# A fused two-layer transformer kernel on one core: a subtraction moved from GpSimd to VectorE, a root moved from GpSimd to ScalarE, and new step orders

## The chip, the cores and the metric

The kernel is written in Bass and runs on one core of a Trainium2 chip. The metric is the device time of one execution in microseconds, lower is better. The five engines (TensorE, VectorE, ScalarE, GpSimd, SyncE) run their own instruction queues in order and meet only at semaphores.

## The reference

`x` has 16 batches of 256 rows with 256 values. Two layers are applied to it, each of the form `x + attention(norm(x)) + ffn(norm(x))`.

- Layer 0: causal attention with 16 heads of 16 values, and a gated feed-forward net of width 704 whose weights are integer codes less 128 times a scale: `down(silu(gate(x)) * up(x))`.
- Layer 1: attention in a latent space. For every head `c = x_h @ Wdkv.T` (64 values) is normalised to mean 0 and variance 1, `c = (c - mu) * rsqrt(var + 1e-5) * g + b`; scores, softmax and values come from `c`. The feed-forward net has a shared gated part (width 192) and 32 experts of width 96, of which each row takes its best 6.

## The kernel before

Nothing of the latent space is formed at its full width: small folded matrices stand in for it. So the normalisation of the keys needs only one number per row and head, `1 / sqrt(variance + eps)`. It is made in the tile `rt2` (128 x 32: two row halves by 16 heads) once a batch. The text calls it the key root. `dve2` multiplies a product from TensorE with the normalised rows (L1330), sums it to `rt2` (L1332), clips it and adds 64 eps (L1334), divides by 64 (L1336); `gp2` raises it to the power -0.5 on GpSimd (L817); `dve2` then spreads it over `rw2` (L1340), TensorE transposes that (L1793), and it scales the keys (L1344) and the values (L1356) of layer 1.

TensorE takes f16 operands. A value that must keep its precision is split in two f16 parts, high and low: ScalarE casts it to the high part, and the low part is the value less the high part. All gated products of the feed-forward nets go this way. There are 288 of them, numbered by `H3`: 6 chunks of layer 0's net a batch ("f"), 2 of the shared net a batch ("s"), and 160 expert units ("u"), each 64 to 128 rows of 256 values. For each one ScalarE does the tanh (L1135), VectorE gates it in two instructions (L1486, and L1490 or L1492) in the tile `th3`, ScalarE casts it to `h3h` (L1140), and GpSimd subtracts to `h3l` (L913); TensorE multiplies both parts with the down weights (L1636, L1633, L1950). `th3`, `h3h` and `h3l` have two buffers each; product n may write `h3l` only when TensorE is through with product n-2.

All work is written as streams of steps, generators that yield at the end of a step: stream 0 is the entry of layer 0 for a batch, 1 its attention, 2 its projection and the entry of layer 1 (with the key root), 3 the feed-forward work of all batches and units, 4 the sum over a row's experts, 7 the routing, 8 the attention of layer 1. Several batches are in flight at once. Which stream an engine serves next is written out by hand in `ORDERS`, one digit a step, for each of the five engines; an engine follows its digits in order, so a step whose data is not there holds up all behind it. The order of the feed-forward uses within stream 3 is `plan`. Its last 34 expert units come after all else; the sum over the experts of the last three batches follows them.

ScalarE uses two functions, Exp and Tanh, beside copies and casts. GpSimd also raises the variances of the two layer norms (L803), issues the scatters and gathers of the expert rows (L889, L933) and does a few sums (L821, L899, L907).

Of the kernel before, what the change touches and what calls it, by code (L numbers as in the profile page):

```python
# [40 lines left out]
def prev(it):  # L41
# [6 lines left out]
        "51111111115555555515555055551005555201111111110281030048111111111121082801008211131111111028800301111811111121"  # L48
        "02881302001181111111208810008331333111111111233333333333323333108833333033003333111111183311133233333313323308"
        "83331333320803303311111111133333321388333331338032333303300111111133113333323883333333108333333033331300333211"  # L50
        "11111113333333321348804333333103038230311331111111333233318833344033138333200033111311111133323334883133433380"
        "31333203300111111113314334338283333333183033334343333313003323301111133111143333438323813330333810330433203311"
        "11111113343333288133333333833313432433333323388333343343333338333333333333333333333333333343343333333333333343"
        "34333333333333334334333333333333834343334444401234678"
    ),
    "gp": (
        "55555553355333553355550555533333323322273300777333333233224007723777333333223233230037773773333332320023237773"
        "77332323233323300777773333332323323323333333007737373373333333333223323233377333007733733332233233332377377337"
        "33333300333332323233233773377337333330033334344344344343443344323232332337733300773373443443344433443232432332"
        "44433773773333730043444344433444232443233342337733773734434334340044344344344322332334423773377337343443443433"  # L60
        "34400434433443443443444433443433323232344443277337773343340043444344433333232324444323443477373737343443444333"
        "33343444324234244334434443773327733734333333333444344344434443433344344344434434443433344344344434434443433344"
        "344344434434443433343444444444444444444444444444444444444440012345677"
    ),
    "act": (
        "75555675567653733353533357335335111151171115115115171150115150173503330733333333727223227727333770011111071131"
        "13011170113133113731113313337888888888888788888888271118112121811132121111200331130111013033333338883288388888"
        "38882238882882888328111338113100111013113011103111131313333333888888888828881118811828281188118212113112138311"
        "38110011033300333233322388838828882888388288888888333838000111101111101111111111118883383383338338833883338333"
        "88233338833238338832833383282333323333333333383331113811311300131331311301131333113033113133130333333333333333"  # L70
        "33333388833883383283838838283233838383283211881138281338113313811383113113313131113133100333033333033303332388"
        "83388323833882388388833233828338838388323833338338111311313331131131131113111113133333333333333388833008383083"
        "88308833808832333883383888332238383323323323338333833333333333333333333331113311311300331311331310118881033113"
        "33113133133338833038338838833388833333883838823883833322333332323332338338311133113111111133113130031130111331"
        "33333033303333333388383238838338833232838833882323882888338883333833833111313133111111131131331131131313333000"
        "33303303888388233838838332832833883233238823833883883833833338333333311131133113113133111111131131888318833838"
        "83880038303883038338038233883282333838333283233333283333333333333333333333333333118883133113311300131881018188"
        "13131333311331133133133033330388338383383333883332838833338833228333823233833233333333111111131111131131333311"
        "33130011313030388830883833388388338338338283338383328823388823233332383338333333311131131133113131133113131313"
        "11331331338838883833883338833383882333888828288832332333323833383333333333333333333333333333333333333333333388"  # L80
        "33888888333333333333333333883333333833333883333333333333333333333338833333333833333333333333338833333333883333"
        "333383333333333333333333333338333333338333333333333330011234788"
    ),
    "dve": (
        "11615516551155611111131131115513135533553550155000550135503533332112232121121127112112112117131131001770070888"
        "08830883888838818838738311113111111111111111811282232822002720072213037077018838888888888888878331133131121121"
        "12121131218112121712318228300300700378807881388738888388188118878131111311311111111111228322200200272832182370"
        "10337887880887388388888888287223211321272311218211111312138113811001710010708878878808888888888718111133133113"
        "13328223211332122373211223118131113113833007003038870773133880338818888838811881381381711311131311131321122123"
        "12183223722238383700313788700738018883880838888388807383232221131312111212183117113111321121831283737388773881"  # L90
        "88888888818838783333003003030303283112213212322372382211381137313178878838871138818811881838181181733380000303"
        "33010333414344343443113841411312142112132114123121213173211822318437338800887700371038808833818838808838783443"
        "43424113221321141213112121813112112117321844413843474378838738873881888880088388173003800304434324442232114432"
        "12321181217231131414121184318141311713378878738888883888888818733434100004340430348034442432242431121328237328"
        "11227313114113117771388183881881818883883881181378443434344003004430344403133443410443434438434432431122132131"
        "21182128311721322711311414131141777888888883883883881800300847480434104434034343383211221321311211212732118122"
        "31184431147114413148378877388888838888188387384443144433333283223244422432738244233844437444323878877838888388"
        "88888873833333333334434443443443444333384434443443443444333344344434434434443333844344438443443444333444444444"
        "444444444444444444444444444001123478"
    ),  # L100
    "pe": (
        "61116116113113111113131313133333113111111111111111001110133103033333333332221111211332311272112111111111300011"
        "81818101883110118831880118831188133881833171831313133111118118131818118118118181818888282118111128112133211232"
        "17111210001011101331880888888888888887833333338328111138118211831188138121811218128281238338312811811371100011"
        "01131011883118810388313811818818818888378331111311313111311813181181188218828118118821182118211281233113118123"
        "18110007110133308883838808888888882878233332338283111288281882188211881181318133811381318117100008811108811818"
        "81810881188188188117181111111833338111333838113383138333823832338113833832381323282332311323113831133131138313"
        "33311811371130001131313188011331131331880331131331880188338838838388383311171831313311313331138113383183283113"
        "28113838238132833282181213811233813811381333811731131131188113133100083188388088383838838830837833033238328338"
        "33821111831812811383121382113383181311821381338132833811371133113131188131311881118818818181831883188338378333"  # L110
# [15 lines left out]
def program(nc, a, out):  # L126
# [29 lines left out]
    with ctx:  # L156
# [736 lines left out]
        def gp3(gp):  # L893
            g = nc.gpsimd
            for use in plan:
                if use[0] == "whole":
# [3 lines left out]
                    yield  # L900
                if use[0] != "in":
                    continue
                n, at = H3[use[1:]], use[1:]
# [1182 lines left out]
```

## Time and profile before

| what | us |
|---|---|
| median of 3 runs | 2054.55 |
| lowest and highest run | 2050.47 and 2056.04 |
| the profiled execution, its own time | 2047.37 |
| its span, first to last instruction | 2045.5 |
| TensorE busy in it | 1523.8 |
| VectorE busy | 1123.0 |
| GpSimd busy | 940.2 |
| ScalarE busy | 877.0 |

The profile is of one execution. A busy share counts the time in which an engine works on an instruction, not in which it is held by one that waits; the waits stand beside the instructions, with what ended them. PE is TensorE, PEld its weight loads, DVE VectorE, ACT ScalarE, POOL GpSimd, SPq the DMA issues of SyncE. The mean granted clock of TensorE was 0.887 of its full 2.4 GHz.

### The profile page before, as it was taken

The page shows a single profiled execution, that of the slowest core. Times are in us where ns is not written, and L with a number is a line of the kernel's source. Part 1 is how long each engine was busy: PE and PEld are TensorE (multiplying, and loading weights), DVE is VectorE, ACT ScalarE, POOL GpSimd, SP SyncE. Part 2 cuts the span into 40 slices and gives each one's busy share as a digit, 9 for nine tenths or more (in the row PEclk, how much of TensorE's full clock was granted, in tenths as well). Part 3 has the DMA queues.
Part 4 walks back from the last instruction along what each step waited for, and adds up shares of the span by engine and source line. Part 5 has one row for each costly group of instructions (what it writes and reads, how often), then busy time and mean ns, then how long its engine had stood idle before and what let it go on. Part 6 is the DMA issues. An engine that isn't in the chain of part 4 may idle for free.

```text
span 2045.5 us, 46039 instructions
## 1 busy us (share of the span) xinstructions
PE 1523.8 (74%) x15344; PEld 1146.5 (56%) x15344; DVE 1123.0 (55%) x2910; ACT 877.0 (43%) x1789; POOL 940.2 (46%) x1246
## 2 busy tenths in 40 slices
PE   3755857787788887887878777797977877788840
PEld 2433545554466666676666656565764666566630
DVE  5565556657555655556465656566555555524332
ACT  2441433353355454553544444453643545355520
POOL 3335062534425154425336455546646456625555
PEclk8777988899899999998999988898998989899975
DMA  6986641413334425353344535364463644546643
GB/s 151 238 212 170 152 112 22 112 45 93 99 87 130 111 90 124 110 125 101 102 105 136 116 122 132 117 144 123 134 150 105 140 127 110 162 125 187 190 141 93
DMA packets 467085, 258.04 MB, mean 126 GB/s; under 512 B 231537, under 2 KB 454321, under 8 KB 466865
## 3 DMA queue, kind: packets, MB, share of 16 engines
q1 hardware_dynamic: 399696, 178.00, 33.8%
q0 software_dynamic: 22784, 54.55, 9.6%
q10 hardware_dynamic: 44384, 22.55, 3.9%
q8 instruction: 140, 2.29, 0.5%
q14 instruction: 81, 0.66, 0.1%
HBM read 127.28 MB, written 127.40 MB: 125 GB/s over the span
## 4 chain that ended last, share of the span: by engine, by line
PE 38%; issue 15%; DVE 14%; POOL 10%; another core or an unknown queue 6%; DMA 5%; SPq 3%; ACT 3%; DVEq 0%; ACTq 0%; POOLq 0%
PE s3r L1636 11%; POOL rt L817 4%; PE s2m L1636 4%; POOL yard L933 2%; PE s3r L1939 2%; PE s1b L1706 2%; PE s3r L1963 2%; SPq L652 2%; DVE th L1486 2%; DMA yard<-y_d,slot 2%; PE s2r L1814 2%; DVE mx L1285 2%; POOL h3l L913 2%; DVE m L1366 1%
## 5 line engine op out<-in xcount | busy, mean ns | idle before, releaser
L913 POOL TENSOR_TENSOR h3l<-th,h3h 96x256 f16<-96x256 f32 (+2 forms) x288 | 199.2, 693 | 602.7 <-ACT h3h L1140 600.1
L1486 DVE SCALAR_TENSOR_TENSOR th<-th,s3r 96x256 f32<-96x256 f32 (+2 forms) x288 | 119.4, 415 | 288.1 <-ACT th L1135 259.8
L933 POOL DMA_INDIRECT yard<-y_d,slot x192 | 192.6, 1003 | 85.8 <-issue 39.9
L1140 ACT CAST h3h<-th 96x256 f16<-96x256 f32 (+2 forms) x288 | 116.5, 405 | 247.8 <-DVE th L1492 124.0
L889 POOL DMA_INDIRECT rows_d<-rows,slot x192 | 188.1, 980 | 67.7 <-issue 66.8
L1366 DVE TENSOR_REDUCE m<-s2r 128x3 f32<-128x384 f32 x256 | 135.4, 553 | 151.2 <-remote 99.3
L1636 PE MATMUL s3r<-yard,xg 128*128 128x128 f16 x1920 | 183.1, 227 | 46.8 <-DVE th L1492 20.6
L1127 ACT COPY yard<-s3r 128x1024 f16<-128x1024 f16 x160 | 162.2, 1014 | 63.1 <-remote 36.4
L1636 PE MATMUL s3r<-yard,xu 128*128 128x128 f16 x1920 | 181.1, 225 | 3.0 <-issue 2.9
L1636 PEld LDWEIGHTS s3r<-yard,xg 128*128 x1920 | 133.0, 101 | 77.4 <-issue 63.6
L1135 ACT ACTIVATE th<-s3r 96x256 f32<-96x256 f32 (+2 forms) x192 | 72.8, 379 | 217.7 <-PE s3r L1636 179.8
L1522 DVE SCALAR_TENSOR_TENSOR yard<-yard,share 128x256 f32<-128x256 f32 x192 | 101.8, 530 | 95.5 <-DMA yard<-y_d,slot 89.1
L1636 PEld LDWEIGHTS s3r<-yard,xu 128*128 x1920 | 135.5, 100 | 12.1 <-issue 3.6
L1090 ACT ACTIVATE weights<-s2r 128x384 f32<-128x384 f32 x256 | 113.9, 489 | 55.6 <-PE s2r L1859 54.5
L1636 PE MATMUL s3r<-xd,h3h 96*128 x640 | 123.0, 287 | 12.4 <-POOL h3l L913 9.0
L1814 PE MATMUL s2r<-stacks 126*128 126x128 f16 (+1 forms) x512 | 94.2, 276 | 46.5 <-issue 26.8
L1963 PE MATMUL s3r<-ident,yard 128*128 128x128 f16 x1280 | 102.6, 225 | 17.5 <-DVE th L1490 9.7
L1027 ACT ACTIVATE weights<-s1a 128x512 f32<-128x512 f32 x144 | 86.3, 599 | 67.0 <-PE s1b L1706 39.8
L1147 ACT COPY yard<-s3r 128x512 f32<-128x512 f32 x160 | 92.9, 581 | 37.4 <-PE s3r L1636 23.6
L817 POOL TENSOR_TENSOR rt<-rt,less_half 128x32 f32<-128x32 f32 x16 | 86.9, 5434 | 40.3 <-DVE rt L1336 40.2
L1963 PEld LDWEIGHTS s3r<-ident,yard 128*128 128x128 f16 x1280 | 86.2, 101 | 29.3 <-issue 25.7
L1285 DVE TENSOR_REDUCE mx<-s1b 128x2 f32<-128x512 f32 x128 | 87.3, 682 | 12.6 <-PE s1b L1688 11.9
(326 smaller groups left out, 3705.0 us busy)
## 6 DMA issues: line engine op xcount, KB each, us to landing
yard<-rows_d SPq DMA_DIRECT2D x160, 256.0 KB
y_d<-yard SPq DMA_DIRECT2D x160, 256.0 KB
rows_d<-share ACTq DMA_DIRECT2D x21, 1024.0 KB, 6.8
part_d<-part SPq DMA_DIRECT2D x32, 512.0 KB, 3.6
stacks<-part_d SPq DMA_DIRECT2D x192, 64.0 KB
land<-part_d SPq DMA_DIRECT2D x96, 64.0 KB
part<-part_d SPq DMA_DIRECT2D x96, 64.0 KB
x<-in_L_attn_x SPq DMA_DIRECT2D x16, 256.0 KB, 2.6
```

The source lines that it names most:

```text
L817: g.tensor_tensor(rt2[:, :, :], rt2[:, :, :], less_half[:, :].unsqueeze(2).to_broadcast([P, T, H]), ALU.pow).then_inc(sem("root2"), 1)
L889: g.indirect_dma_start(rows_d[k % 2][:, :], bass.IndirectOffsetOnAxis(ap=slot4[:, it, t, j:j + 1], axis=0), rows2[:, t, :, :].rearrange("p ...
L913: g.tensor_tensor(h3l[0:m, n % 2, :], th3[0:m, n % 2, :], h3h[0:m, n % 2, :], ALU.subtract).then_inc(sem("low3"), 1)
L933: g.indirect_dma_start(got4[:, n % RING4, :], None, y_d[k][:, :], bass.IndirectOffsetOnAxis(ap=slot4[:, b, t, j:j + 1], axis=0)).then_inc( ...
L1127: s.copy(xt3[:, r % 2, :, :, :].rearrange("p i g n -> p (i g n)"), bk[:, :].bitcast(F16)).then_inc(empties3(use), 1)
L1140: s.copy(h3h[0:m, n % 2, :], th3[0:m, n % 2, :]).then_inc(sem("high3"), 1)
L1285: v.tensor_reduce(mx1[:, h, :], two(bk), AX.X, ALU.max).then_inc(empties1(u), 1)
L1366: v.tensor_reduce(m32[:, h, :], bk[:, 0:3 * P].rearrange("p (c n) -> p c n", n=P), AX.X, ALU.max).then_inc(empties2(u), 1)
L1486: v.scalar_tensor_tensor(h, h, 1.0, bk[0:m, 0:2 * P], ALU.add, ALU.mult).then_inc(sem("gate3"), 1)
L1636: ins = nc.tensor.matmul(bk, lhs[i][k], rhs[j][k], start=first, stop=last)
L1814: mm(bk[:, P * j:P * j + P * (j + 1)], query(qst2, h, OPEN)[:, P * j:P * j + P], key(kst2, h, OPEN)[:, 0:P * (j + 1)], start=j == 0, stop= ...
L1963: ins = nc.tensor.transpose(bk[:, 512 * i + P * k:512 * i + P * k + P], rows3[:, r % 2, i, P * k:P * k + P], ident16[:, :])
```

## The change

Three things, and new orders for all five engines.

- The low part of the gated products is made by VectorE, as a step of its own behind the gate's step, in place of GpSimd.
- The key root: VectorE's division by 64 goes (ScalarE's activation scales by 1/64 itself), ScalarE takes the square root in place of GpSimd's power, and VectorE takes the reciprocal.
- `ORDERS`: GpSimd has 304 steps fewer (288 low parts, 16 roots), VectorE 288 more, ScalarE 16 more. All five strings are new. `plan` is the same.

```diff
@@ ORDERS @@
-    "sp": ( ... 713 steps ... ), "gp": ( ... 729 ... ), "act": ( ... 1823 ... ), "dve": ( ... 1576 ... ), "pe": ( ... 2197 ... )
+    "sp": ( ... 713 steps ... ), "gp": ( ... 425 ... ), "act": ( ... 1839 ... ), "dve": ( ... 1864 ... ), "pe": ( ... 2197 ... )
@@ gp2 @@
-            gp.wait_ge(*event("var2_made", it, 1))
-            g.tensor_tensor(rt2[:, :, :], rt2[:, :, :], less_half[:, :].unsqueeze(2).to_broadcast([P, T, H]), ALU.pow).then_inc(sem("root2"), 1)
-            yield
@@ gp3 @@
-                m = rows_of(at)
-                gp.wait_ge(*event("high3", None, n + 1))
-                if n >= 2:
-                    gp.wait_ge(*weighed3(n - 2))
-                g.tensor_tensor(h3l[0:m, n % 2, :], th3[0:m, n % 2, :], h3h[0:m, n % 2, :], ALU.subtract).then_inc(sem("low3"), 1)
-                yield
@@ act2, between the copy of x2h and the routing's Exp @@
+            act.wait_ge(*event("var2_made", it, 1))
+            s.activation(rt2[:, :, :], rt2[:, :, :], ACT.Sqrt, scale=1.0 / L).then_inc(sem("root2"), 1)
+            yield
@@ dve2 @@
-            v.tensor_scalar(rt2[:, :, :], rt2[:, :, :], 0.0, L * EPS, ALU.max, ALU.add).then_inc(sem("var2_scaled"), 1)
-            dve.wait_ge(*event("var2_scaled", it, 1))
-            v.tensor_scalar(rt2[:, :, :], rt2[:, :, :], 1.0 / L, None, ALU.mult).then_inc(sem("var2_made"), 1)
+            v.tensor_scalar(rt2[:, :, :], rt2[:, :, :], 0.0, L * EPS, ALU.max, ALU.add).then_inc(sem("var2_made"), 1)
             yield
             dve.wait_ge(*event("root2", it, 1))
+            v.reciprocal(rt2[:, :, :], rt2[:, :, :]).then_inc(sem("rs2_made"), 1)
+            dve.wait_ge(*event("rs2_made", it, 1))
             dve.wait_ge(*event("row_low", it, 1))
             v.tensor_copy(rw2, rt2[:, :, :].unsqueeze(3).to_broadcast([P, T, H, HD])).then_inc(sem("rs2_made"), 1)
@@ dve3, behind the gate @@
+                    dve.wait_ge(*event("high3", None, n + 1))
+                    if n >= 2:
+                        dve.wait_ge(*weighed3(n - 2))
+                    v.tensor_tensor(h3l[0:m, n % 2, :], h, h3h[0:m, n % 2, :], ALU.subtract).then_inc(sem("low3"), 1)
+                    yield
@@ pe2 @@
-            pe.wait_ge(*event("rs2_made", it, 1))
+            pe.wait_ge(*event("rs2_made", it, 2))
```

## Rows read from the trace of the kernel before

**Rows 1.** The page's busy time by engine, with instruction counts.

```profile
PE 1523.8 (74%) x15344; PEld 1146.5 (56%) x15344; DVE 1123.0 (55%) x2910; ACT 877.0 (43%) x1789; POOL 940.2 (46%) x1246
```

**Rows 2.** The page's chain that ended last, by engine and by line.

```profile
PE 38%; issue 15%; DVE 14%; POOL 10%; another core or an unknown queue 6%; DMA 5%; SPq 3%; ACT 3%; DVEq 0%; ACTq 0%; POOLq 0%
PE s3r L1636 11%; POOL rt L817 4%; PE s2m L1636 4%; POOL yard L933 2%; PE s3r L1939 2%; PE s1b L1706 2%; PE s3r L1963 2%; SPq L652 2%; DVE th L1486 2%; DMA yard<-y_d,slot 2%; PE s2r L1814 2%; DVE mx L1285 2%; POOL h3l L913 2%; DVE m L1366 1%
```

**Rows 3.** Windows by stage: length, then busy us of each engine, PEclk, DMA, GB/s.

```profile
500.00:1000.00 500.00, 410.64 (x4339) 319.28 (x4338) 284.33 (x754) 237.69 (x490) 197.61 (x297) 0.93 0.38 105
1000.00:1500.00 500.00, 405.61 (x4237) 311.70 (x4234) 291.15 (x765) 235.85 (x489) 258.92 (x334) 0.92 0.49 129
1750.00:1980.00 230.00, 175.29 (x1936) 139.70 (x1936) 80.93 (x190) 109.83 (x206) 111.78 (x142) 0.93 0.56 164
```

**Rows 4.** The tile rt: durations ns (min/median/max), and who waited for its writers.

```profile
L1336 DVE TENSOR_SCALAR rt<-rt x16: 181/182/425, 157.5 to 1727.5; 128x32 f32<-128x32 f32 x16
L817 POOL TENSOR_TENSOR rt<-rt,less_half x16: 5419/5424/5513, 157.7 to 1728.0; 128x32 f32<-128x32 f32 x16
...
  DVE xn L1340: 75.5, 16
```

**Rows 5.** Timeline of one key root: start, us, what, idle before and its releaser.

```profile
809.42 0.18 DVE L1336 TENSOR_SCALAR rt<-rt 128x32 f32<-128x32 f32 x1
...
809.68 5.42 POOL L817 TENSOR_TENSOR rt<-rt,less_half 128x32 f32<-128x32 f32 x1 [5.79 <-DVE rt L1336]
...
815.14 0.43 DVE L1340 COPY xn<-rt 128x512 f32<-128x512 f32 x1 [4.94 <-POOL rt L817]
...
816.22 0.11 PEld L1686 LDWEIGHTS s1b<-kst,qst 126*128 126x128 f16 x2 [4.80 <-DVE mx L1285]
```

**Rows 6.** Windows, each root's start to 3 us behind its end: first, last, sum.

```profile
157.74:166.18 8.44, 4.49 (x52) 3.77 (x50) 3.58 (x16) 1.10 (x3) 5.43 (x1) 0.89 0.36 103
...
1728.00:1736.44 8.44, 3.98 (x48) 3.38 (x46) 3.28 (x16) 3.27 (x7) 7.91 (x4) 0.89 0.30 93
sum 135.04, PE 67.90 PEld 51.02 DVE 52.31 ACT 34.85 POOL 99.12; mean PE 4.24 PEld 3.19 DVE 3.27 ACT 2.18 POOL 6.20
```

**Rows 7.** By line, xcount | busy us, mean ns | idle before; then the stage window of h3l.

```profile
L913 POOL TENSOR_TENSOR h3l<-th,h3h 96x256 f16<-96x256 f32 (+2 forms) x288 | 199.2, 693 | 602.7 <-ACT h3h L1140 600.1 <-issue 1.1
...
L1140 ACT CAST h3h<-th 96x256 f16<-96x256 f32 (+2 forms) x288 | 116.5, 405 | 247.8 <-DVE th L1492 124.0 <-DVE th L1490 109.7 <-issue 9.8
...
1750.00:1980.00 230.00, 33.31 (x47) 0.93 0.56 164
```

**Rows 8.** Nearest prices: lines L1537, L1396, L1239, L1070, then ScalarE's first two instructions.

```profile
L1537 DVE TENSOR_TENSOR shd<-stacks,shd x1: 407/407/407, 67.1 to 67.1; 64x256 f16<-64x256 f32 x1
...
L1396 DVE RECIPROCAL sc<-el x16: 552/553/554, 163.8 to 1734.1; 128x64 f32<-128x64 f32 x16
...
L1239 DVE RECIPROCAL rc<-s2r x32: 235/248/258, 243.0 to 1940.2; 128x16 f32<-128x16 f32 x32
...
L1070 ACT ACTIVATE el<-s2m x16: 223/223/230, 159.0 to 1728.8; 128x64 f32<-128x64 f32 x16
...
0.80 1.28 ACT L1157 ACT_TABLE_LOAD   x1 [0.80 <-PEq L2076]
6.56 1.47 ACT L1157 CAST wqkv<-yard 128x1536 f16<-128x1536 f32 x1 [4.48 <-DMA yard<-in_L_attn_w_qkv]
```

**Rows 9.** TensorE's waits from 180 to 1750 us: us in total, times, longest.

```profile
PE s1b L1726 <- ACT weights L1027: 28.1, 16, 6.1
...
PE s1b L1686 <- DVE mx L1285: 14.0, 10, 4.8
```

**Rows 10.** Timeline of one expert unit among the last 34.

```profile
1859.94 0.40 ACT L1140 CAST h3h<-th 96x256 f16<-96x256 f32 x1 [0.94 <-DVE th L1492]
...
1860.43 0.67 POOL L913 TENSOR_TENSOR h3l<-th,h3h 96x256 f16<-96x256 f32 x1 [3.60 <-ACT h3h L1140]
...
1862.76 0.10 PEld L1636 LDWEIGHTS s3r<-xd,h3l 96*128 96x128 f16 x1
...
1863.08 0.42 DVE L1486 SCALAR_TENSOR_TENSOR th<-th,s3r 96x256 f32<-96x256 f32 x1 [3.17 <-issue]
```

More of the change, by code:

```diff
@@ new lines @@
+        "31883333330330013333111111121138333331332338803333303300331331111118233111333333323388013330330803331113311111"
+        "31123333333334433123088333303300331331111113823111333441333323883330331483230400331111311111333233338833133344"
+        "30383310302301111131131413348332338333333013833303003333133111111121133333833314423383333330133323380330011313"
+        "11114113342333388331333333334338413332348433323383333333333333333333333383333333333333334334333333333333433433"
+        "33333383333433433333333333333433433333334444401234678"
@@ L69 @@
[L69 to L73, printed above, removed]
@@ new lines @@
+        "30113701331133113137331111311778888888788888882118188881181212181182211321112110011313031303303333333332888888"
+        "88228882882328888888280080338301111013113311313111113311313113313888888882888882882888881122831211121181133001"
+        "13811010113113013133333333388828888888282888828288328811181233181001381101110111011111188833388333323383388333"
+        "32332883338388332388233238883388323333383333333833383333111333333311330033113333133311333113113301331313113313"
+        "31333030333333333332333333888388233283888828388233882382388338833833330038338311131133331131131311031133101131"
@@ new lines @@
+        "13310331333333333333333333333233888388388822883838822883281188138832813138333118113133113331131333003303330333"
+        "11303113133133333333333333333388823388388832882338388322883382883388238333833383333333311313113311311100110111"
+        "00111113313333338883338838333388338833833883333238838333883388223833323233233323833311138113113331310031311301"
+        "11033333110331311333133333333333333333888388238888832823883388283338832111332881181323181313138131311331333113"
+        "11131333000333303308883288333888388332328388328832833883238832833333833338333333331113311331133111311331131331"
@@ new lines @@
+        "13111331330088888088808833380883388332838838833833232833338323232332333333333333333333333333333331113130013110"
+        "11101888311031133331133118831338133883388383883883338388338833823833328233333223211111332131313131333113113133"
+        "31313133131313333333330033303303330328883388338883883282388338823828832882383333833383333333333111311331313311"
+        "31333111313313331131133131333888338838338838838388388328888882282382333233233333333333333333333333333333333333"
+        "33333333333333333333333333333333888333388333383883338833338333333333883333883383388338833338333333333333333383"
@@ new lines @@
+        "38228330370077887881888888888188118178111111111333333233322233323323821373323112333321313813131833333333003730"
+        "03303337377333883388310333338130333883883883883883838723111323211231311212111213138721321311330032003831103833"
+        "33733388377730388180338333138811388318883883118313871131311313123131221121123238127323228383373333388300880078"
+        "70387330833813033338313883118818838338713113131313132322232332382731322323811383111137131313388388300877373380"
+        "03388088088880881783131131331313413143431131314343383124443223443231141231321142137332831232384344334003743004"
@@ L902, in gp3 @@
                     continue
-                n, at = H3[use[1:]], use[1:]
+                at = use[1:]
                 if at[0] == "s" and at[2] == 0:
```

101 lines of the change are left out of this document (40 added, 61 removed), and 4 rows, old and new, of the table PER.

## The prediction

> **What bounds the kernel now.** I read the busy shares first: TensorE leads with 74%, VectorE has 55%, and GpSimd and ScalarE are below half [rows 1]. No engine is full, so I went on to the chain that ended last. TensorE has 38% of it, VectorE 14%, GpSimd 10%, ScalarE 3%, and 15% is issue [rows 2]. GpSimd's part matters here: the key root's power alone is 4%, some 82 us, and the low part h3l is 2%, some 41 us.
>
> The windows by stage split the run. From 500 to 1500 us, where batches overlap, TensorE is busy 0.82 of the time, VectorE 0.57, ScalarE 0.47 [rows 3]. From 1750 to 1980 us only expert units are left, and VectorE falls to 0.35. Behind 1980 us is the last sum over experts, which has no gated product and no root.
>
> So in the overlapped stage TensorE is the nearest to a bound, and the rest is in-order queues waiting for one another. What the change is worth is what it does to the queues of VectorE and ScalarE in that stage.
>
> **The root: what goes.** The power takes 5.42 us on GpSimd, 16 times, and VectorE stands still for 75.5 us in front of the copy L1340 that needs it [rows 4]. The timeline shows the damage: VectorE idles 4.94 us, the score maxima L1285 stand behind it, and TensorE, whose bank they free, waits 4.80 us [rows 5].
>
> How much of a stall turns into time? In the 16 windows from a root's start to 3 us behind its end, 135.0 us in all, TensorE was busy 67.9 us [rows 6]. At the 0.82 of the stage around it would have been busy 110.7. It lost 42.8 us of work, which at 0.82 is 52 us of time, for 75.5 us of VectorE's stall: 0.69 us per us. I use that ratio as what a microsecond costs in which VectorE's queue is held at its worst place. These windows include the lower clock there (PEclk 0.89 in both shown, against 0.93 and 0.92 in the stage) [rows 3, 6].
>
> **The root: what comes.** VectorE loses one instruction of 0.18 us [rows 4] and gains a reciprocal of 128x32. The same operation takes 0.248 us at 16 elements and 0.553 at 64 [rows 8]; between them, 0.35 us at 32. Net +0.17 us, 3 us in 16 batches. ScalarE gains a square root of 128x32; its activation of 128x64 takes 0.22 us [rows 8], so about 0.20, 3 us in all.
>
> The trace has one table load in the whole run, 1.28 us, although Exp and Tanh alternate all the way [rows 8]: they share a table. I take it that Sqrt does not, which no row shows. Then each batch has two more loads, one ahead of the root and one ahead of the next Exp or Tanh: 32 x 1.28 = 41 us of ScalarE.
>
> VectorE's wait is then: 0.08 us hop to ScalarE (as from L1336 to L817 in [rows 5]), 0.3 us for what ScalarE is at, 1.28 load, 0.20 root, 0.05 back: 1.9 us against 75.5/16 = 4.7. That saves 2.8 x 16 = 45 us of stall, less 3 for the reciprocal: 42. At 0.69 it is **-29 us**. Bounds: if the load runs ahead of the wait, as the first one did (it ended at 2.08, the data came at 6.56 [rows 8]), the wait is 0.6 us and the gain 63 x 0.69 = 44 us; if ScalarE comes late by an exponential or two and has to empty first, the wait is 3.3 us and the gain is 14 us. I take the middle, since ScalarE is busy about half of the stage.
>
> The Trainium skill (ScalarE: Activation LUTs, "What ACT_TABLE_LOAD costs" and "Table sets") states that exp and tanh are in one set and sqrt in another, that a switch is a 1283 ns load plus a drain of about 1380 ns, and so advises against alternating exp and sqrt. The 1.28 us row agrees with the load; no run here shows the drain yet. By its 2.66 us the root's wait would be 3.3 us and ScalarE's extra 85 us in place of 41, and that sum would give about 20 to 30 us more than mine.
>
> **The tables' cost to ScalarE's own queue.** 41 + 3 = 44 us are added to 877. Behind them stand the exponentials, and TensorE waits for those already, 28.1 us at one line alone [rows 9]. Lower price: ScalarE's share of the chain, 3% of 2045 = 61 us for 877 busy, 0.07 us per us. Upper: 0.69, as for a held queue. ScalarE is idle half of the stage, so nearer the lower end: 0.25, **+11 us** (3 to 30).
>
> **The low part: what moves.** GpSimd loses 199.2 us [rows 7]. VectorE has done exactly this operation once, f32 less f16 to f16 of 64x256 from SBUF, in 0.407 us [rows 8], and 288 of them are 117 us. 47 lie in the stage of units alone [rows 7], where VectorE next has a gate 2 us later and TensorE reads h3l 1.7 us after GpSimd has finished it [rows 10]: these cost nothing. 241 x 0.407 = 98 us remain in the overlapped stage.
>
> The new step waits for ScalarE's cast in VectorE's queue, where before GpSimd had the wait (600.1 us of it, free of charge [rows 7]). In the new order of VectorE, of the 244 low steps ahead of the end stage, 49 follow their gate at once, 99 with one step between, 96 with more. At once means a hop, the cast's 0.405 us and a hop, 0.5 us each, 25 us; with one step of about 0.39 us (1123 us by 2910 instructions [rows 1]) some 0.2 us are left, 20 us. Behind the waiting instruction stand the score maxima, and TensorE waits for them (14.0 us at one line already [rows 9]).
>
> So VectorE's queue gets 98 + 45 = 143 us longer in a stage in which it is 0.57 busy. Lower price: its share of the chain over its busy time, 14% of 2045 = 286 by 1123, 0.25 us per us, gives 36. Upper: 0.69, gives 99. New orders can place much of it well, but the waits are of the same kind as the root's, so I take 0.4: 57 us. Against it stands the chain's 41 us of L913, which come back at 0.407/0.693: -17. Together **+40 us** (19 to 82). With no cast waits at all it would be +8.
>
> GpSimd's gathers and scatters no longer stand behind low parts. This I cost at nothing: the gathers wait for saved units, and the last 66 us hold no low part.
>
> **Sum.** -29 + 11 + 40 = +22 us on the profiled execution: own time 2047.4 to 2069, span 2045.5 to 2067. That execution was 7 us faster than the median shown; on the median the sum gives 2076, and I write 2075. SyncE's and TensorE's digits are new too; what they do as such I can't price and it widens the range by some 10 us each way.
>
> **Rivals.**
>
> *A, the root wins (faster).* The load runs ahead of the root's wait, and the low parts sit in VectorE's idle time. For it: VectorE is idle 0.43 of the stage, and all 16 powers lie on the chain. Against: 148 of 244 low steps have at most one step between. -44 + 3 + 8 = -33: 2022 us. It decides when a microsecond of VectorE's added work costs under about 0.25 and the root's wait is under 1.5 us.
>
> *B, they cancel.* The root's wait is as in my sum, VectorE's price is the chain's 0.25: -27 + 8 + 19 = 0: 2054 us.
>
> *C, the tables cost more than their loads.* ScalarE reaches the root late, empties, loads, and its exponentials stand behind. The wait is 3.3 us, the root saves 14, ScalarE's extra is 64 us (a further 0.6 us, one exponential's length, per switch) at 0.69, 44 us, and the low part +40: +70, 2125 us. For it: the order has Exp and Tanh on both sides of nearly every root. Against: ScalarE has 3% of the chain. The Trainium skill's drain, cited above, is this mechanism.
>
> **Chances.** My forecast 0.38 (its own range 2062 to 2095), A 0.30, B 0.18, C 0.14. The range that holds 8 in 10 is 2020 to 2115: it takes in A's centre and half of C. Within 0.3% (6 us, about what the runs shown, 2050 to 2056, can tell from no change) is B, 0.18; slower is the forecast and C, 0.52; faster is A, 0.30.
>
> **What would show it.** Right: 33 table loads of 1.28 us; VectorE's wait before the reciprocal near 1.9 us, 30 us in all against 75.5; h3l on VectorE at 0.41 us and 117 us; VectorE near 1240 us busy, GpSimd near 654, ScalarE near 921; waits of VectorE for the cast L1140 of 30 to 60 us; TensorE's share of the stage down from 0.82. Wrong: if no further table load stands in the trace the root's gain nears 44 us; if VectorE's waits for the cast are small and TensorE's waits for L1285 shrink, A holds; if TensorE waits for exponentials behind the loads more than 60 us, C.

## The result, and the profile after

The changed kernel takes 2027.54 us at the median of 4 runs (2020.76 to 2031.42), the kernel before on the same chip 2055.3 us (2050.47 to 2058.01). The ratio is 0.9864, with an interval from 0.983 to 0.9898: **28 us faster**. The prediction had said 2075 us and slower; its range of 2020 to 2115 holds the time. The profiled execution's own time is 2020.76 us, its span 2018.9.

Busy time and the chain that ended last, of the changed kernel's page, for comparison with [rows 1, 2]:

```profile
PE 1508.2 (75%) x15344; PEld 1127.1 (56%) x15344; DVE 1205.5 (60%) x3198; ACT 916.0 (45%) x1837; POOL 664.5 (33%) x942
...
PE 40%; DVE 19%; issue 10%; another core or an unknown queue 9%; DMA 6%; ACT 5%; SPq 3%; POOL 2%; DVEq 0%; ACTq 0%; POOLq 0%
PE s3r L1634 12%; PE s2m L1634 4%; PE s3r L1937 3%; DVE m L1359 3%; PE s3r L1961 2%; DVE mx L1278 2%; DMA yard<-y_d,slot 2%; PE s2r L1854 2%; DVE th L1479 2%; SPq L651 2%; PE s1b L1704 2%; POOL yard L923 1%; PE s3r L1948 1%; PE s2r L1812 1%
```

The work moved as foreseen (ScalarE 921, GpSimd 654 and VectorE 1240 were named; VectorE has 1205.5). GpSimd's share of the chain fell from 10% to 2%, and VectorE's rose from 14% to 19%.

The tile rt after (durations min/median/max; then who waited for its writers), which answers to [rows 4]:

```profile
L1057 ACT ACTIVATE rt<-rt x16: 229/229/231, 155.8 to 1696.0; 128x32 f32<-128x32 f32 x16
L1330 DVE RECIPROCAL rt<-rt x16: 341/345/353, 156.9 to 1696.3; 128x32 f32<-128x32 f32 x16
L1333 DVE COPY xn<-rt x16: 426/427/474, 157.3 to 1696.7; 128x512 f32<-128x512 f32 x16
...
  ACT rt L1057: 7.1, 2
  DVE rt L1330: 5.6, 6
```

VectorE's 16 waits for the root, 75.5 us before, are 6 waits of 5.6 us in all. The prediction had 30. The timeline of one root after (start, us, what, idle before) shows why, beside [rows 5]:

```profile
911.68 0.59 ACT L1140 COPY yard<-s3r 128x512 f32<-128x512 f32 x1
...
911.93 0.18 DVE L1327 TENSOR_SCALAR rt<-rt 128x32 f32<-128x32 f32 x1
912.02 0.41 DVE L1490 TENSOR_TENSOR h3l<-th,h3h 96x256 f16<-96x256 f32 x1
912.29 1.28 ACT L1057 ACT_TABLE_LOAD   x1
...
912.63 0.62 DVE L1239 TENSOR_TENSOR on<-s2r,rc 128x64 f32<-128x64 f32 x4
...
913.58 0.23 ACT L1057 ACTIVATE rt<-rt 128x32 f32<-128x32 f32 x1
...
913.83 1.28 ACT L1063 ACT_TABLE_LOAD   x1
913.84 0.35 DVE L1330 RECIPROCAL rt<-rt 128x32 f32<-128x32 f32 x1 [0.59 <-ACT rt L1057]
914.23 0.43 DVE L1333 COPY xn<-rt 128x512 f32<-128x512 f32 x1
...
1692.42 1.28 ACT L1057 ACT_TABLE_LOAD   x1
...
1696.04 0.23 ACT L1057 ACTIVATE rt<-rt 128x32 f32<-128x32 f32 x1 [2.34 <-DVE rt L1327]
```

The new order puts a low part and a few short steps between the variance and the reciprocal, so the load and the root lie beside VectorE's work. Table loads are there as foreseen, 33 of 1.283 us, two for each root; in the last batch the load ran ahead of the wait, 2.3 us before the data came.

Windows after: two of the 16 from a root's start, their sum, then the stage (length, busy us of TensorE, its weight loads, VectorE, ScalarE, GpSimd, PEclk, DMA, GB/s), beside [rows 3, 6]:

```profile
155.83:164.27 8.44, 6.53 (x61) 4.89 (x59) 5.82 (x23) 2.57 (x5) 0.00 (x0) 0.94 0.61 174
...
1696.07:1704.51 8.44, 6.90 (x81) 5.70 (x78) 6.65 (x29) 5.70 (x12) 0.66 (x1) 0.99 0.51 159
sum 135.04, PE 115.82 PEld 88.89 DVE 101.77 ACT 98.70 POOL 17.07; mean PE 7.24 PEld 5.56 DVE 6.36 ACT 6.17 POOL 1.07
...
500.00:1000.00 500.00, 412.91 (x4488) 319.95 (x4487) 308.57 (x844) 259.68 (x524) 126.23 (x215) 0.95 0.43 114
1000.00:1500.00 500.00, 404.37 (x4310) 309.60 (x4308) 326.70 (x887) 250.82 (x511) 184.91 (x268) 0.92 0.48 127
```

TensorE is busy 115.8 of the 135.0 us around the roots, where it had 67.9 [rows 6]: the hole is gone. In the two stage windows its busy share is that of before, 0.82, but they hold 8798 of its instructions in place of 8576 [rows 3], 2.6% more in the same 1000 us, at a granted clock of 0.95 in place of 0.93 in the first. The busy share hid the gain; the count of instructions shows it.

The low part after (the tile h3l: what wrote it, and what VectorE waited for), then TensorE's waits for the score maxima:

```profile
L1490 DVE TENSOR_TENSOR h3l<-th,h3h x288: 360/416/1920, 72.0 to 1943.2; 96x256 f16<-96x256 f32 x80, 128x256 f16<-128x256 f32 x56, 64x256 f16<-64x256 f32 x8
...
  ACT h3h L1133: 50.5, 78
```

```profile
PE s1a L1684 <- DVE mx L1278: 7.7, 12, 1.5
...
PE s1b L1684 <- DVE mx L1278: 2.2, 6, 0.9
```

The cast waits are 50.5 us, the 30 to 60 foreseen, and yet TensorE waits less for the maxima, 2.2 us where one line had 14.0 [rows 9].

### The profile page after: what moved, and what is told of

It is laid out like the page before. It is cut to its first block, busy times and chain, and to the rows that moved or that the text cites. A ratio compares the mean times of both kernels' runs of the same rounds, so it can differ in the third digit from the quotient of the medians.

```text
span 2018.9 us, 46071 instructions
## 1 busy us (share of the span) xinstructions
PE 1508.2 (75%) x15344; PEld 1127.1 (56%) x15344; DVE 1205.5 (60%) x3198; ACT 916.0 (45%) x1837; POOL 664.5 (33%) x942
## 4 chain that ended last, share of the span: by engine, by line
PE 40%; DVE 19%; issue 10%; another core or an unknown queue 9%; DMA 6%; ACT 5%; SPq 3%; POOL 2%; DVEq 0%; ACTq 0%; POOLq 0%
PE s3r L1634 12%; PE s2m L1634 4%; PE s3r L1937 3%; DVE m L1359 3%; PE s3r L1961 2%; DVE mx L1278 2%; DMA yard<-y_d,slot 2%; PE s2r L1854 2%; DVE th L1479 2%; SPq L651 2%; PE s1b L1704 2%; POOL yard L923 1%; PE s3r L1948 1%; PE s2r L1812 1%
## 5 line engine op out<-in xcount | busy, mean ns | idle before, releaser
L1359 DVE TENSOR_REDUCE m<-s2r 128x3 f32<-128x384 f32 x256 | 134.1, 551 | 133.6 <-remote 82.3
L1490 DVE TENSOR_TENSOR h3l<-th,h3h 96x256 f16<-96x256 f32 (+2 forms) x288 | 125.3, 435 | 54.0 <-ACT h3h L1133 50.5
L802 POOL TENSOR_TENSOR mv<-mv,less_half 128x2 f32<-128x2 f32 x32 | 24.1, 752 | 395.8 <-DVE mv L1218 395.6
L1520 DVE SCALAR_TENSOR_TENSOR yard<-yard,share 128x256 f32<-128x256 f32 x192 | 95.1, 495 | 86.1 <-DMA yard<-y_d,slot 77.2
L1812 PEld LDWEIGHTS s2r<-stacks 126*128 126x128 f16 x512 | 44.4, 103 | 110.1 <-DVE m L1359 51.1
L1854 PE MATMUL s2r<-stacks 128*128 128x256 f16 (+1 forms) x512 | 74.4, 254 | 34.6 <-ACT yard L1092 13.1
```

Source lines behind the costliest of these rows:

```text
L1359: v.tensor_reduce(m32[:, h, :], bk[:, 0:3 * P].rearrange("p (c n) -> p c n", n=P), AX.X, ALU.max).then_inc(empties2(u), 1)
L1490: v.tensor_tensor(h3l[0:m, n % 2, :], h, h3h[0:m, n % 2, :], ALU.subtract).then_inc(sem("low3"), 1)
L1812: mm(bk[:, P * j:P * j + P * (j + 1)], query(qst2, h, OPEN)[:, P * j:P * j + P], key(kst2, h, OPEN)[:, 0:P * (j + 1)], start=j == 0, stop= ...
L1854: mm(ring2[u % 2][:, at:at + S - P * j], key(kst2, h, FULL)[:, P * j:P * j + P], query(qst2, h, FULL)[:, P * j:S], start=j == 0, stop=Fals ...
```

## The experiments

Each was timed in 5 rounds beside the kernel before on the same chip. Microseconds are the ratio's distance from 1 by 2054.55. Two theories stood against each other at first: *prices*, that my terms had the wrong size, and *orders*, that the new orders made the gain. "Old orders" are those of before with the moved steps put in and nothing else moved: the low parts at the times where they had run, the root's step on ScalarE right ahead of the routing's Exp.

**The root.** `cheap_pow` is the kernel before with a multiplication for the power, so the root's value is left out:

```diff
-  g.tensor_tensor(rt2[:, :, :], rt2[:, :, :], less_half..., ALU.pow).then_inc(sem("root2"), 1)
+  g.tensor_tensor(rt2[:, :, :], rt2[:, :, :], less_half..., ALU.mult).then_inc(sem("root2"), 1)
```

> The kernel before with the power on GpSimd replaced by a multiplication of the same shape (the key root's value is left out). Nothing else changes, the orders stay. Root theory (a held VectorE queue costs 0.69 us per us): VectorE's wait before L1340 falls from 75.5 us to about 8 us, and the time by 45 us (35 to 55), to a ratio of 0.978. Orders theory (the gain of the change came from the new orders): under 15 us. Low-part theory (the gain came from the low part): under 15 us.

Measured: 0.9586 [0.9551, 0.9621], 85 us faster. The tile rt of that kernel (the durations, then who waited):

```profile
L817 POOL TENSOR_TENSOR rt<-rt,less_half x16: 238/239/336, 156.6 to 1651.5; 128x32 f32<-128x32 f32 x16
...
  POOL rt L817: 1.1, 3
```

VectorE's wait went from 75.5 to 1.1 us, 74 us for 85 us of time: **1.14 us per us, not 0.69**. The same edit takes 83 us off GpSimd (16 times 5.424 less 0.239), about what the chain in [rows 2] had for the power, 4% or 82 us. This run doesn't separate what VectorE's stall cost from what GpSimd's held queue cost.

`root_only` is the kernel before with the diff's hunks of gp2, act2, dve2 and pe2 alone, in the old orders. `root_no_sqrt` is the same with no table switch; it leaves the root out:

```diff
-  s.activation(rt2[:, :, :], rt2[:, :, :], ACT.Sqrt, scale=1.0 / L).then_inc(sem("root2"), 1)
+  s.activation(rt2[:, :, :], rt2[:, :, :], ACT.Identity, scale=1.0 / L).then_inc(sem("root2"), 1)
```

> The kernel before with the key root alone moved to ScalarE with a reciprocal; in the orders GpSimd's root steps are dropped and a step for ScalarE is put right ahead of the routing's Exp, all else stays. Root theory: 32 more table loads, VectorE's wait 10 to 30 us instead of 75.5, and 25 to 45 us faster, as much as the whole change or more (ratio about 0.983). Orders theory: about 0 to 10 us. Low-part theory: under 10 us.

> The root moved alone in the old orders, with Identity in place of Sqrt (the square root is left out), so that no table is switched. If the loads cost in the old orders what lies between the cheap power (0.9586) and the root moved alone (0.9774): a ratio near 0.960, 30 to 40 us under the root moved alone. If they are hidden as in the changed kernel (where leaving them out gave 0.9867 against 0.9864): 0.975 to 0.980, and the difference comes from where ScalarE's step stands.

Measured: `root_only` 0.9774 [0.9735, 0.9814], 46 us faster; `root_no_sqrt` 0.9635 [0.9604, 0.9666], 75 us. VectorE's wait for the root, first of `root_only`, then of `root_no_sqrt`:

```profile
  ACT rt L1064: 20.8, 13
```

```profile
  ACT rt L1064: 8.0, 8
```

The root away from GpSimd is worth 75 us, and the table loads take 29 back. By 1.14 the 12.8 us of longer wait would be 15 of these (an estimate); 14 are left for ScalarE's own queue, where I had 11.

`after_no_sqrt` makes the same edit in the changed kernel.

> The changed kernel with Identity in place of Sqrt (the square root is left out), so that no table is switched; the orders and all else stay. If the 32 loads (41 us of ScalarE) are hidden, as ScalarE's 0.07 us per us of the chain has it: 0 to 5 us faster than the changed kernel (2028). If they hold ScalarE's queue as the root held VectorE's: 25 to 40 us faster (about 1995), which is what lies between the cheap power (1970) and the root moved alone (2007).

Measured: 0.9867 [0.9842, 0.9892] against 0.9864 for the changed kernel. In the new orders the 32 loads cost nothing that shows; the intervals would hide some 9 us.

`pow_late` is the kernel before with VectorE's order sorted anew, so that the copy (L1340) comes about 4 us later by the profile's times. In half of the batches that puts 1 to 3 more steps ahead of it, and in all 224 of VectorE's 1576 steps stand in another place.

> The kernel before with both parts on GpSimd; in VectorE's order the step that needs the root is put 4 us later by the profile's times, as far as the other engines' orders allow (another 0 to 3 steps go ahead of it in half of the batches). If VectorE's order was what made the power a stall: 15 to 40 us faster than before. If the chain over the power itself decides, since TensorE's order goes through the root: under 10 us.

Measured: 1.0089 [1.0055, 1.0123], 18 us slower, though VectorE's wait fell from 75.5 to 68.6 us. A step put off shortens the wait and can lengthen the chain through the root. With so many steps moved the run doesn't show that this is the cause; it shows that a shorter wait there is no gain by itself.

**The low part.** `low_only` is the kernel before with the hunks of gp3 and dve3 alone; `both_simple` has both moves, in the old orders.

> The kernel before with the low part alone moved to VectorE; its steps stand in VectorE's order where GpSimd began them in time in the profile before, all other digits stay. Root theory: slower by 8 to 40 us (my prediction had 40, the result of the change points to 10 to 20), ratio about 1.007. Low-part theory (GpSimd's slow and blocked low part was the loss): faster by 15 to 30 us. Orders theory: slower by more than 30 us, since it takes new orders to hide it.

> The kernel before with both moves and the two simple edits of the orders together, without the new orders. Root theory: the sum of the two, 15 to 30 us faster, near the change itself (ratio 0.986 to 0.993). Orders theory: no faster than before or slower, the whole gain is missing. Low-part theory: faster by 25 us, of which the low part gives most.

Measured: 1.0249 [1.0214, 1.0283], 51 us slower, and 1.0035 [1.0012, 1.0058]. So the low part costs 51 us alone and 54 on top of the root, and the new orders, from `both_simple` to the changed kernel, give back 1.7%, **35 us**. That comes out of two comparisons, each with before, and it takes in whatever is poor in my own placing of the steps: against a better placing in the old orders it would be less. From `root_only` to the changed kernel, low part and new orders together, it is 18 us of loss.

`after_low_twice` makes each low part a second time on VectorE; `after_low_tiny` and `both_low_tiny` make 8 of its 256 columns. The rest is not zero as the expectation has it: the zeroing stands ahead of the start of the kernel, which uses the same memory for constants, and what that wrote stays.

```diff
+  v.tensor_tensor(h3l[0:m, n % 2, :], h, h3h[0:m, n % 2, :], ALU.subtract).then_inc(sem("twice3"), 1)
+  dve.wait_ge(*event("twice3", None, n + 1))
   v.tensor_tensor(h3l[0:m, n % 2, :], h, h3h[0:m, n % 2, :], ALU.subtract).then_inc(sem("low3"), 1)
...
-  v.tensor_tensor(h3l[0:m, n % 2, :], h, h3h[0:m, n % 2, :], ALU.subtract).then_inc(sem("low3"), 1)
+  v.tensor_tensor(h3l[0:m, n % 2, 0:8], h[:, 0:8], h3h[0:m, n % 2, 0:8], ALU.subtract).then_inc(sem("low3"), 1)
```

> The changed kernel with every low part computed twice on VectorE, the second behind the first; the orders stay. It prices VectorE's work in its queue: 288 x 0.42 = 121 us and some 0.05 us between. At 0.25 us per us (VectorE's share of the chain): 30 us slower than the changed kernel. At 0.4, my prediction's price: 50 us. At 1.0, as the root's stall was worth by the cheap power: 120 us.

> The changed kernel with a low part of 8 columns of 256 on VectorE (the other columns are left zero), so that the step, its waits and its place stay and 0.26 us of its work go, 75 us in all. At the 0.24 us per us that computing it twice gave: 18 us faster than the changed kernel, a ratio near 0.977. At 0.4: 30 us, 0.971.

> Both moves in the old orders (both_simple, 1.0035) with the same low part of 8 columns. If the low part's cost in the old orders is VectorE's work: 18 to 30 us faster than both_simple, 0.989 to 0.995, most of the way back to the root alone (0.9774). If it is that its steps stand badly in the old orders, where they wait for casts and hold what is behind: under 10 us faster, above 0.998.

Measured: twice 1.0007 [0.9982, 1.0031], 29 us above the changed kernel for 120 us more of VectorE's busy time, 0.25 us per us. Tiny 0.9837 [0.9805, 0.9869] and 0.9994 [0.9975, 1.0013], 6 and 8 us below their parents for about 70 us less, 0.1 us per us; the 6 are not clear of the intervals, the 8 barely. The work's price is about 0.1 to 0.25, not the 0.4 that I took.

`after_no_cast_wait` and `both_no_cast_wait` make the low part as the gated value less itself (zero), so VectorE reads no cast and waits for none; TensorE waits for it.

```diff
-  dve.wait_ge(*event("high3", None, n + 1))
+  dve.wait_ge(*emptied3(use))
...
-  v.tensor_tensor(h3l[0:m, n % 2, :], h, h3h[0:m, n % 2, :], ALU.subtract).then_inc(sem("low3"), 1)
+  v.tensor_tensor(h3l[0:m, n % 2, :], h, h, ALU.subtract).then_inc(sem("low3"), 1)
@@ pe3, three places @@
+  pe.wait_ge(*event("high3", None, n + 1))
```

> The changed kernel with a low part that does not read the cast (the gated value less itself, so the low part is zero), so that VectorE waits only for its own gate; TensorE waits for the cast itself. It prices the wait for the cast, 50.5 us in 78 waits in the changed kernel. If these waits cost what they last: 30 to 50 us faster than the changed kernel, a ratio near 0.965. If they lie in slack: under 10 us, 0.982 to 0.986.

> The kernel before with both moves in the old orders (2065.73 us, ratio 1.0035), but each low part is computed as the gated value minus itself (zero), so VectorE does not read the cast and does not wait for ScalarE there; TensorE waits for the cast itself. The low part is left out of the result. Theory A, the waits of VectorE for the cast (47.9 us, 72 of them) are what the low part costs in the old orders: 25 to 45 us faster, a ratio of 0.982 to 0.991. Theory B, GpSimd's emptied queue: about 1.003. Theory C, the low part's place in VectorE's order: 0.998 to 1.003, since the steps stay where they are.

Measured: 0.9836 [0.9807, 0.9865] against 0.9864, and 1.0036 [1.0016, 1.0056] against 1.0035. **The cast waits, 45 us in my sum, cost about 6 us in the new orders, which the intervals can't tell from nothing, and nothing in the old ones.**

**GpSimd's emptied queue.** VectorE's 120 us of work are 12 to 30 of the 54 us by these prices, the waits nothing. The rest had no owner. `both_gp_busy` is `both_simple` with GpSimd doing a subtraction of the same size on constants, behind the same cast, at each old place of a low part:

```diff
+  gp.wait_ge(*event("high3", None, H3[use[1:]] + 1))
...
+  g.tensor_tensor(spare[0:m, :], sd_row[0:m, :], wgate[0:m, 0, 0:E], ALU.subtract).then_inc(sem("idle_low"), 1)
+  yield
```

> The kernel before with both moves in the old orders (2065.73 us, ratio 1.0035), and GpSimd keeps the queue that it had with the low part: in its place it does a subtraction of the same size on constants into a spare tile. Theory B, that scatters and gathers which now run earlier disturb the rest: 25 to 45 us faster, a ratio of about 0.985. Theory A, the waits for the cast: unchanged at about 1.003, since these stay. Theory C, the place of the steps in VectorE's order: unchanged too.

Measured: 0.9905 [0.9888, 0.9921]. **288 useless instructions on GpSimd make the kernel 27 us faster.** From `root_only` (0.9774) to it is VectorE's side of the low part, 27 us; from it to `both_simple` is the emptied queue, 27 us. The two are not quite separate: with GpSimd's subtractions beside them VectorE's own low parts take 0.505 us in the mean in place of 0.435, and VectorE is busy for 40 us more than in `both_simple`. VectorE runs its instructions in the same order in both, so I set them side by side: the later start does not grow evenly but jumps, 12.3, 8.8, 8.7, 6.8 and 6.6 us at five steps of L1359. The timeline of `both_simple` at the first of these:

```profile
1665.20 0.96 POOL L885 DMA_INDIRECT rows_d<-rows,slot  x1 [0.30 <-issue]
1665.39 0.42 DVE L1485 TENSOR_TENSOR th<-s3r,th 96x256 f32<-96x256 f32 x1
...
1671.53 0.96 POOL L885 DMA_INDIRECT rows_d<-rows,slot  x1 [0.30 <-issue]
1672.79 0.97 POOL L885 DMA_INDIRECT rows_d<-rows,slot  x1 [0.30 <-issue]
1673.13 0.60 ACT L1017 ACTIVATE weights<-s1b 128x512 f32<-128x512 f32 x1 [8.22 <-remote]
...
1673.78 0.61 PE L1724 MATMUL s1b<-qst,kst 128*128 128x256 f16 x2 [8.90 <-ACT weights L1017]
...
1678.06 0.56 DVE L1359 TENSOR_REDUCE m<-s2r 128x3 f32<-128x384 f32 x1 [12.24 <-issue]
```

And the window of that stretch, then the one of `both_gp_busy` at the same place:

```profile
1665.85:1673.10 7.25, 0.00 (x0) 0.00 (x0) 0.00 (x0) 0.00 (x0) 5.42 (x7) 0.50 0.27 94
```

```profile
1636.55:1643.80 7.25, 4.58 (x42) 3.10 (x40) 2.47 (x6) 3.06 (x5) 5.84 (x7) 1.00 0.39 129
```

For 7.25 us no instruction of TensorE, VectorE or ScalarE stands in the trace. The views name no instruction that held them: VectorE's next one has "issue" as its releaser, ScalarE's has "remote", an event that they put down to nothing in the trace. GpSimd issues scatters all the while, 1.27 us from one to the next; TensorE's clock falls to 0.50, its lower level of 1.2 GHz.

The trace's semaphore events go further than the views. The ends of TensorE's matmuls in a profile are modelled, but the event by which a matmul tells the others that it is through is a record of its own. ScalarE starts at 1673.13, 0.08 us behind the event of a matmul whose end stands at 1661.91. In the longest stretch of the changed kernel (shown below) the events of four matmuls whose ends stand at 1719.40 to 1720.73 come at 1731.63 to 1731.81, and ScalarE and VectorE, which wait for two of them, start at 1731.65 and 1731.70. Elsewhere such an event lies 0.01 us behind the end (the median, for each of the three engines). **So in the still stretches VectorE and ScalarE wait for TensorE, whose matmuls report up to 12 us late there.** In `both_simple` 141 of TensorE's events are 1.5 to 20 us late, and in 139 of these delays GpSimd issues a gather or scatter. All eight kernels of the table below have the same 15344 matmuls in their traces, so missing records are not the reason.

With low-part steps between some scatters (`both_gp_busy`, at 1641.39) the same stretch runs on. It does so already over the four scatters from 1636.41 to 1640.41, which follow one another as closely, so scatters in a row are not enough by themselves.

```profile
1640.41 0.96 POOL L889 DMA_INDIRECT rows_d<-rows,slot  x1 [0.30 <-issue]
1641.39 0.69 POOL L912 TENSOR_TENSOR spare<-sd_row,wgate 96x256 f16<-96x256 f32 x1
1642.25 0.99 POOL L889 DMA_INDIRECT rows_d<-rows,slot  x1 [0.17 <-issue]
```

I counted such stretches ahead of the last gate in each trace: over 1.5 us without an instruction of the three engines, with at least two indirect issues under way in them. Beside them stands the time in which an event of TensorE was due by its matmul's end and over 1.5 us late, overlaps counted once.

| kernel | ratio | still stretches | us in them | us with a late event |
|---|---|---|---|---|
| before | 1 | 10 | 33.9 | 202 |
| `root_only` | 0.9774 | 8 | 33.0 | 208 |
| `both_gp_busy` | 0.9905 | 9 | 27.8 | 198 |
| `low_only` | 1.0249 | 16 | 57.9 | 237 |
| `both_simple` | 1.0035 | 15 | 64.9 | 240 |
| `both_no_cast_wait` | 1.0036 | 13 | 50.3 | 230 |
| `both_low_tiny` | 0.9994 | 12 | 40.6 | 226 |
| the changed kernel | 0.9864 | 13 | 54.3 | 266 |

They come with the emptied queue: the three kernels in which GpSimd has a subtraction for each product have the least of both, and between `both_simple` and `both_gp_busy` it is 37 us of still stretches for 27 us of time. But they don't follow the time one to one: `both_low_tiny` has 24 us less of them than `both_simple` and gained 8. The changed kernel still has 54 us, the longest of them here:

```profile
1720.80:1731.60 10.80, 0.00 (x0) 0.00 (x0) 0.00 (x0) 0.00 (x0) 8.06 (x9) 0.63 0.42 148
```

**The new orders with the old placement.** `after_root_gp`, `after_low_gp` and `after_both_gp` give the root, the low part, or both back to GpSimd in the changed kernel, each step where its data had been ready. The other engines keep their order, less or plus the moved steps. GpSimd's own order is sorted anew, so its other steps change places too, which the expectations don't say. `after_low_gp2` and `after_both_gp2` put GpSimd's scatters 8 and 16 us later in its order.

> The changed kernel with the root back on GpSimd (the power), its steps in GpSimd's order at the times at which ScalarE began the square root; all other digits stay. Additive theory (root, low part and orders each have their own worth): 45 to 55 us slower than the changed kernel, about 2077. Rival, the new orders hide a slow root: under 20 us slower.

> The changed kernel with the low part back on GpSimd, its steps in GpSimd's order at the times at which VectorE began them; VectorE's low steps go, all other digits stay. Additive theory: 40 to 55 us faster than the changed kernel, 1975 to 1988. Fit theory (the new orders only make up for what the low part costs): 15 to 25 us faster, the same as the root moved alone in the old orders (2007).

> The new orders alone: root and low part both on GpSimd as in the kernel before, in the changed kernel's orders. Additive theory: 25 to 40 us faster than the kernel before (about 2022). Fit theory: the orders are worth nothing without the low part on VectorE, 2045 to 2070.

> As after_low_gp (the changed kernel with the low part back on GpSimd), but GpSimd's scatter steps are put 8 and 16 us later in its order, so that fewer low parts stand behind them (in after_low_gp the low parts began 715 us in all after their casts, in the kernel before 224). If the orders are good in themselves and only GpSimd's queue spoiled after_low_gp: faster than the changed kernel, 1975 to 2010. If the new orders suit only a low part on VectorE: still slower than the kernel with the root moved alone (2007 on a chip where before is 2058).

> As after_both_gp (the new orders with root and low part on GpSimd), with the scatter steps 8 and 16 us later in GpSimd's order. Against after_low_gp2 it adds the 5.4 us power: 80 to 100 us slower than that one by the root theory. Orders good in themselves: below the kernel before, 2030 to 2050; orders that suit only the new places: above it.

Measured: 1.0498 [1.0471, 1.0525], 1.1035 [1.1006, 1.1064], 1.1302 [1.1269, 1.1335], 1.0608 [1.0572, 1.0645] and 1.0909 [1.0871, 1.0946]. Of the last four I can say only that GpSimd's queue is bad in them: in `after_low_gp` TensorE's costliest waits are for low parts that stand behind scatters.

```profile
PE s3r L1636 <- POOL h3l L910: 118.8, 21, 18.5
PE s3r L1950 <- POOL h3l L910: 115.4, 23, 21.1
```

So they do not price the low part. `after_root_gp` is 130 us slower than the changed kernel (45 to 55 were expected), where the root was worth 46 us in the old orders, but it is not the root's price alone: GpSimd comes to 6 of the 16 powers 2 to 11 us late, 30 us in all, and VectorE's wait for the root is 98.8 us. The run fits orders that are made for a root that is there in 2 us, and doesn't show it by itself.

## Why the prediction was wrong

My terms in the order of the sum, and what the runs gave:

| term | predicted | measured |
|---|---|---|
| root, had it no loads | -44 | -75 in the old orders (`root_no_sqrt`) |
| loads, in VectorE's wait and in ScalarE's queue | +15 and +11 | +29 in the old orders, 0 in the new |
| root in all | -18 | -46 in the old orders (`root_only`) |
| low part | +40, for the new orders | +54 in the old orders (+51 alone) |
| new orders | not priced, 10 either way | -35 |
| low part and new orders together | +40 | +18 |
| sum | +22 | -28 |

**The root's price was too low.** The step that failed is "0.69 us per us". I took it from TensorE's idle time up to 3 us behind each root; `cheap_pow` has 1.14. What that window missed was not measured, but the chain that I had read first had it: 82 us for the power, and `cheap_pow` gave 85. The stall was also shorter than the 30 us I left to it, 20.8 us in `root_only` and 5.6 after. With the loads the root should have been -46, not -18. That alone turns the sum from +22 to -6.

**The orders had no term.** "What they do as such I can't price" was true, but 10 us was no bound that any row gave, and against the moved steps put into the old orders they did 35 us. My +40 for the low part was meant for the new orders; low part and orders together came to +18. That alone brings the sum to 0, and both errors together make the 50 us between +22 and -28. I had counted in the new order of VectorE how soon each low part follows its gate, and had not looked at what stands between the variance and the reciprocal, which is where the loads now lie.

**The low part was near in size for the wrong reasons.** +54 in the old orders is within my bounds of 19 and 82. But the cast waits (45 of my 143 us) cost nothing that shows, VectorE's work costs 0.1 to 0.25 us per us rather than 0.4, and half of the cost is a step of which I had written "This I cost at nothing", that GpSimd's gathers and scatters no longer stand behind low parts. It is 27 us in the old orders.

**The tables.** The count, the 1.28 us and their place were right. The Trainium skill (ScalarE: Activation LUTs, "What ACT_TABLE_LOAD costs") adds a drain of about 1380 ns to each switch. Here the rows show the load beginning 0.02 us behind ScalarE's last work in the timeline above and the root starting 0.01 us behind the load, and `after_no_sqrt` shows that the switches cost nothing there. By the drain in the Trainium skill they would have held ScalarE for 44 us more, an estimate from its figure; the rows show no such time, and they decide.

**Rival A** was close in size (-33) and in kind in the new orders: the load beside other work, the root's wait under 1.5 us, VectorE's work at about 0.25. It had a chance of 0.30. Not one of my cases held that the emptied queue costs anything. That the root alone would beat the whole change lay in my own terms (-18 against +22), and it does: `root_only`, 0.9774 [0.9735, 0.9814], is the fastest kernel here that computes everything, 0.9% below the changed kernel, whose interval is from 0.983 to 0.9898.

**Open.** Why TensorE's events come late while GpSimd issues scatters. The loading of instructions is not it: in the two longest stretches of `both_simple`, 7.3 and 8.4 us, no packet of the instruction queues moved. Whether the 1.14 is VectorE's stall or GpSimd's held queue. Whether the changed kernel would gain from spaced-out scatters, and whether `root_only` would gain from orders of its own, was not tried. How the 35 us of the new orders divide between the hidden loads (29 us in the old orders, 0 in the new) and the rest was not measured either; the two numbers suggest that the loads are most of it.

## What to carry to other kernels

A stall is not priced by its length alone. Here one on the chain cost 1.14 us per us, and the cast waits cost nothing that shows; a window that ended just behind the stall gave too low a price, and the power's share of the chain that ended last gave nearly the right one. Work taken off an engine is not free either: ask what its queue then does earlier, above all where it issues indirect DMAs in a row. When a change comes with new orders, run its parts in the old ones: here one half of the change was worth more than the whole.

## What the runs showed of the hardware that I had not expected

- While GpSimd issues scatters or gathers 1.27 us apart, the events of TensorE's matmuls at times come up to 12 us behind the ends that the profile gives them, and VectorE and ScalarE stand still until then, for up to 10.9 us. 288 idle subtractions on GpSimd made this rarer (65 to 28 us of still stretches) and the kernel 27 us faster.
- "Remote" and "issue" in front of an idle engine can be TensorE's late event: the views look for a matmul that ended then and find none.
- A table switch showed nothing but the load of 1.283 us: it began 0.02 us behind ScalarE's last work, the function 0.01 us behind it, and the load can run before the wait of the function it serves (1692.42 against 1696.04).
- GpSimd's power of 128x32 takes 5.42 us, its multiplication of the same shape 0.239 us, 23 times less.
